# A fused sequence model on one core: the attention core rewritten with values computed first and all loops unrolled

## What is computed

```python
q = x @ Wq; k = x @ Wk; v = x @ Wv
attn = softmax(einsum('btd,bTd->btT', q, k) * scale)        # within each 64-token sequence
attn_out = einsum('btT,bTd->btd', attn, v) @ Wp + bp
cms_out = gelu(attn_out @ cW1 + cb1) @ cW2 + cb2 + target_embed
modifier = gelu(concat([attn_out, cms_out]) @ mW1 + mb1) @ mW2 + mb2
out = clip(x + cms_out + modifier, 0, 1)
```

## Time and profile before

| | us |
|---|---|
| median of 3 runs (2616.24 to 2621.03) | 2616.32 |
| profiled execution, its time | 2620.1 |
| profiled execution, its span | 2618.4 |
| TensorE busy | 2477.1 (95%) |
| TensorE weight loads busy | 2049.8 (78%) |
| VectorE busy | 1048.2 (40%) |
| ScalarE busy | 922.3 (35%) |
| GpSimd busy | 377.6 (14%) |

### The profile page before, as it was taken

The page is one execution under the profiler, slowest core; times in us unless marked ns, Lnnn a source line. Parts: engine busy times, 40 slices in busy tenths (PEclk is TensorE's granted clock), DMA queues, the critical chain, the costliest instruction groups (busy, mean ns, idle before and its releaser), DMA issues. The chain is left out here.

```text
span 2618.4 us, 29174 instructions
## 1 busy us (share of the span) xinstructions
PE 2477.1 (95%) x11376; PEld 2049.8 (78%) x11376; DVE 1048.2 (40%) x1434; ACT 922.3 (35%) x1242; POOL 377.6 (14%) x294
## 2 busy tenths in 40 slices
PE   5888999999999999999999999998999999969995
PEld 4765788888878888888788888887888888758884
DVE  4544333422244333222433342224333322357776
ACT  3544333322234333222334332223333222246663
POOL 2673000000000000000000000000000000029887
PEclk9999999999999999999999999999999999989997
DMA  5444011021120110211201111102111111063243
GB/s 185 153 169 177 33 48 48 32 80 48 48 81 33 50 46 33 80 48 48 97 33 48 48 71 58 48 32 81 43 41 56 50 48 50 34 225 137 81 137 129
DMA packets 41676, 195.64 MB, mean 75 GB/s; under 512 B 5746, under 2 KB 5746, under 8 KB 24836
## 3 DMA queue, kind: packets, MB, share of 16 engines
q1 hardware_dynamic: 35844, 152.68, 16.8%
q0 software_dynamic: 5760, 41.95, 4.0%
HBM read 163.16 MB, written 31.46 MB: 74 GB/s over the span
## 5 line engine op out<-in xcount | busy, mean ns | idle before, releaser
L1181 DVE TENSOR_TENSOR h_lo<-g,h_hi 128x512 fp32r<-128x512 f32 x256 | 177.4, 693 | 756.3 <-ACT h_hi L1089 756.3
L57 PE MATMUL bank<-h_hi,w_hiB 128*128 128x512 f32 x1152 | 449.2, 390 | 11.7 <-DVE h_lo L1158 11.7
L59 PE MATMUL bank<-h_hi,w_loB 128*128 128x512 f32 x1152 | 448.4, 389 | 0.0
L58 PE MATMUL bank<-h_lo,w_hiB 128*128 128x512 f32 x1152 | 448.2, 389 | 0.0
L1086 ACT ACTIVATE g<-bank,bias_cols 128x512 f32<-128x512 f32 x256 | 176.5, 689 | 630.0 <-PE bank L59 393.2
L59 PE MATMUL bank<-o_hi,w_loA 128*128 128x512 f32 x768 | 298.9, 389 | 0.0
L57 PE MATMUL bank<-o_hi,w_hiA 128*128 128x512 f32 x768 | 298.8, 389 | 0.0
L58 PE MATMUL bank<-o_lo,w_hiA 128*128 128x512 f32 x768 | 298.8, 389 | 0.0
L1028 ACT ACTIVATE w_hiB<-w_raw 128x2048 fp32r<-128x2048 f32 x37 | 71.0, 1920 | 565.5 <-PE bank L59 565.5
L57 PEld LDWEIGHTS bank<-h_hi,w_hiB 128*128 128x128 f32 x1152 | 216.2, 188 | 58.2 <-issue 6.7
L59 PEld LDWEIGHTS bank<-h_hi,w_loB 128*128 128x128 f32 x1152 | 216.2, 188 | 45.5
(11 more groups left out here) (210 smaller groups left out, 4213.8 us busy)
## 6 DMA issues: line engine op xcount, KB each, us to landing
w_raw<-in_units_a SPq DMA_DIRECT2D x32, 1024.0 KB, 4.8
w_raw<-in_units_b SPq DMA_DIRECT2D x32, 1024.0 KB, 4.8
w_raw<-in_units_c SPq DMA_DIRECT2D x16, 1024.0 KB, 4.8
w_raw<-in_w_packed SPq DMA_DIRECT2D x30, 512.0 KB, 4.1
w_raw<-in_rows_packed SPq DMA_DIRECT2D x20, 512.0 KB, 4.5
x_tok<-x SPq DMA_DIRECT2D x16, 512.0 KB, 6.6
x<-stage SPq DMA_DIRECT2D x32, 256.0 KB, 2.8
first_gain<-in_rows_packed SPq DMA_DIRECT2D x10, 512.0 KB, 4.5
```

The costliest lines, as they stand in the source:

```text
L57: pe.matmul(out, lh, rh, start=(i == 0), stop=False)
L58: pe.matmul(out, lh, rl, start=False, stop=False)
L59: last = pe.matmul(out, ll, rh, start=False, stop=(i == len(terms) - 1))
L1181: v.tensor_tensor(h_lo[:, j, cols(n)], g[q % 2][:], h_hi[:, j, cols(n)].bitcast(F32), ALU.subtract).then_inc(hlo_done, 1)
```

## The change

The core computes the same. What differs:

- **Values first.** The product with `fold_v` is taken of the transposed input, tile by tile (`value`, eight product tiles per block, tokens as rows), and ScalarE evicts each result over the token tile in `x_tok`. `attend` then multiplies these values with the probabilities, and its result is the output itself: `a_hi`, `a_lo` and the output product go, and `attended` makes `o_hi` and `o_lo`.
- **Order on TensorE.** Value tiles stand between queries, scores and the transposes of the probabilities; both halves are attended one behind the other.
- **Next block.** In the last chunk of blocks 0 to 2, the next block's 32 transposes stand among the output tiles (after the first and after the fourth) and use banks 0 to 3 only; transposes 4 to 7 wait for the low halves of tiles 0 to 3. Query 0 of the next block follows the output tiles, then four of the eight tiles of final transposes, the first value tile, and the other four. Final transposes use banks 4 to 7, and wait for all accumulations. The query waits for the low halves of all eight tiles.
- **Raw input.** It is evicted to `xr`, in the space of `o_hi`, because `acc` is still in use. GpSimd copies it to `acc` when the final transposes of the block before are done; ScalarE waits for these copies before it writes `o_hi`.
- **Queues.** On ScalarE and VectorE the evictions and splits of the next block stand in the last chunk, between the splits of slots A, C and B. On SyncE the stores of a block stand behind the first two weight loads of the next block; the wait for a block's stores moves to VectorE, ahead of the first hidden chunk. In block 3 the last three weight loads and splits, which nothing uses, are left out.
- **Loops.** All hardware loops of the core are unrolled, and addresses are constants.

The core of the diff, with what stays the same left out:

```diff
+    V_BANK = (0, 1, 5, 6, 0, 1, 2, 3)
+    S_BANK = (4, 7)
...
+        xr = sb("xr", [P, KD, SBT], at=places["o_hi"])
...
-        a_hi = h_hi[:].rearrange("p k n -> p (k n)")[:, 0:KD * 512].rearrange("p (k n) -> p k n", k=KD)
-        a_lo = h_lo[:].rearrange("p k n -> p (k n)")[:, 0:KD * 512].rearrange("p (k n) -> p k n", k=KD)
...
-        probsT = sb("probsT", [P, HT, P])
+        probsT = [sb(f"probsT{n}", [P, HT, P]) for n in range(NH)]
...
+            def store(s):
+                for t in range(TT):
+                    sp.wait_ge(fin_done, TT * s + t + 1)
+                    sp.dma_start(dst[s * SBT + t * P:s * SBT + (t + 1) * P, :], stage[:, t, :]).then_inc(stored[t % 2], 16)
...
+            for s in range(SB):
+                more = s < SB - 1
                 load_a(s, 1, units_a[0])
                 load_bc(s, 1, 1, units_b[0])
+                if s:
+                    store(s - 1)
                 for c in range(CH):
                     load_a(s, 2 + c, units_a[1 + c])
                     load_bc(s, 2 + c, 1, units_b[1 + c])
                 for c in range(CH):
+                    if c < CH - 1 or more:
+                        load_a(s, 2 + CH + c, units_a[1 + CH + c] if c < CH - 1 else fold_m)
+                        load_bc(s, 2 + CH + c, 1 + c, units_c[(c + 1) % CH])
+                        load_bc(s, 2 + CH + c, 2 + c, units_b[1 + CH + c] if c < CH - 1 else fold_v)
                     if more and c == 0:
                         sp.wait_ge(sum_ready, TILES * s + TILES)
                         load_x(s + 1)
...
+            def transposes(s, tiles):
+                for t in tiles:
                     if t % XT == 0:
                         pe.wait_ge(x_in[t // XT], 16 * s + 16)
+                    if t >= 4:
+                        pe.wait_ge(xlo_done, TT * s + t - 3)
+                    elif s:
+                        pe.wait_ge(gelu_done, HTILES * s - 3 + t)
                     for k in range(KD):
+                        last = pe.transpose(bank[t % 4][:, k * P:(k + 1) * P], x_tok[:, t, k * P:(k + 1) * P], ident[:])
                     last.then_inc(tr_done, 1)
+            def query(s, n):
+                pe.wait_ge(lo_done["A"], NA * s + 1)
+                pe.wait_ge(xlo_done, TT * s + TT)
+                if n:
+                    pe.wait_ge(v_done, TT * s + 2)
+                for m in range(KD):
+                    product(pe, bank[m][:], unit_terms("A", m, xc_hi, xc_lo, n)).then_inc(y_mm, 1)
+            def value(s, t):
+                pe.wait_ge(lo_done["B"], NBU * s + 1)
+                if t < 2:
+                    pe.wait_ge(y_done, TILES * s + t + 1)
+                elif t >= 4:
+                    pe.wait_ge(y_done, TILES * s + KD + t - 3)
+                elif s:
+                    pe.wait_ge(fin_done, TT * s - 4 + t)
+                product(pe, bank[V_BANK[t]][:], [((xc_hi[:, k, tile(t)], xc_lo[:, k, tile(t)]),
+                                                  (w_hi["B"][:, k, :], w_lo["B"][:, k, :])) for k in range(KD)])\
+                    .then_inc(v_mm, 1)
+            def scores(s, n):
+                pe.wait_ge(y_done, TILES * s + KD * (n + 1))
+                if s:
+                    pe.wait_ge(fin_done, TT * s - 3 + 3 * n)
+                for i in range(HT):
+                    for k in range(KD):
+                        last = pe.matmul(bank[S_BANK[n]][:, tile(i)], yT[:, k, tile(i)], xr[:, k, tile(HT * n + i)],
+                                         start=(k == 0), stop=(k == KD - 1))
+                last.then_inc(s_mm, 1)
+            def turn_probs(s, n):
+                pe.wait_ge(probs_done, 2 * NH * s + 2 * (n + 1))
+                for i in range(HT):
+                    last = pe.transpose(bank[S_BANK[n]][:, tile(i)], probs[:, i, :], ident[:])
+                last.then_inc(pt_mm, 1)
+            def attend(s, n):
+                pe.wait_ge(pt_done, NH * s + n + 1)
+                pe.wait_ge(v_done, TT * s + TT)
+                for k in range(KD):
+                    for i in range(HT):
+                        last = pe.matmul(bank[4 * n + k][:, tile(i)], x_tok[:, HT * n + i, tile(k)],
+                                         probsT[n][:, i, :], start=True, stop=True)
+                    last.then_inc(av_mm, 1)
...
+            def finish(s, tiles):
+                pe.wait_ge(acc_done, HTILES * (s + 1))
+                for t in tiles:
+                    if t >= 4:
+                        pe.wait_ge(fin_done, TT * s + t - 3)
                     for m in range(KD):
...
+            transposes(0, range(TT))
+            query(0, 0)
+            value(0, 0)
+            for s in range(SB):
+                value(s, 1)
+                scores(s, 0)
+                query(s, 1)
+                value(s, 2)
+                value(s, 3)
+                scores(s, 1)
+                turn_probs(s, 0)
+                for t in range(4, TT):
+                    value(s, t)
+                turn_probs(s, 1)
+                attend(s, 0)
+                attend(s, 1)
+                for c in range(CH):
+                    condition(s, c)
+                    out_tiles(s, c, range(TILES))
+                for c in range(CH, 2 * CH - 1):
+                    mix(s, c)
+                    out_tiles(s, c, range(TILES))
+                c = 2 * CH - 1
+                mix(s, c)
+                if s < SB - 1:
+                    out_tiles(s, c, range(1))
+                    transposes(s + 1, range(4))
+                    out_tiles(s, c, range(1, 4))
+                    transposes(s + 1, range(4, TT))
+                    out_tiles(s, c, range(4, TILES))
+                    query(s + 1, 0)
+                    finish(s, range(4))
+                    value(s + 1, 0)
+                    finish(s, range(4, TT))
+                else:
+                    out_tiles(s, c, range(TILES))
+                    finish(s, range(TT))
...
+            def valued(s, t):
+                act.wait_ge(v_mm, TT * s + t + 1)
+                act.activation(x_tok[:, t, :], bank[V_BANK[t]][:], ACT.Copy).then_inc(v_done, 1)
...
+            def attended(s, n):
+                for k in range(KD):
+                    act.wait_ge(av_mm, TILES * s + KD * n + k + 1)
+                    act.activation(o_hi[:, k, cols(n)], bank[4 * n + k][:], ACT.Identity, bias=bp[:, k:k + 1]).then_inc(ohi_done, 1)
...
+                valued(s, 0)
+                valued(s, 1)
+                softmax(s, 0)
+                queried(s, 1)
                 split("A", NA * s + 2)
+                valued(s, 2)
+                valued(s, 3)
+                turned(s, 0)
+                softmax(s, 1)
+                for t in range(4, TT):
+                    valued(s, t)
+                turned(s, 1)
+                act.wait_ge(acc_init, KD * s + KD)
+                attended(s, 0)
+                attended(s, 1)
                 split("B", nb + 3)
...
+                for c in range(CH):
+                    chunk(s, c + CH)
+                    if c < CH - 1:
+                        split("A", NA * s + c + 3 + CH)
+                        split("C", nb + 2 * c + 4 + CH)
+                        act.wait_ge(out_mm, HTILES * s + TILES * (c + CH) + TILES)
+                        split("B", nb + 2 * c + 5 + CH)
+                    elif s < SB - 1:
+                        split("A", NA * s + c + 3 + CH)
+                        transposed(s + 1, range(4))
+                        split("C", nb + 2 * c + 4 + CH)
+                        transposed(s + 1, range(4, TT))
+                        act.wait_ge(out_mm, HTILES * s + TILES * (c + CH) + TILES)
+                        split("B", nb + 2 * c + 5 + CH)
+                        queried(s + 1, 0)
...
+                softmax(s, 0)
                 split("A", NA * s + 2)
+                softmax(s, 1)
+                attended(s, 0)
+                attended(s, 1)
                 split("B", NBU * s + 2)
...
+                    accumulate(s, c, cms, range(TILES))
                     split("B", NBU * s + c + 3)
                 for r in range(TILES):
                     n, m = r // KD, r % KD
                     v.wait_ge(chi_done, TILES * s + r + 1)
                     v.tensor_tensor(xc_lo[:, m, cols(n)], cms[:, m, cols(n)], xc_hi[:, m, cols(n)].bitcast(F32),
                                     ALU.subtract).then_inc(clo_done, 1)
...
+                for c in range(CH):
+                    hidden_lo(s, c + CH)
+                    if c == 0:
+                        v.wait_ge(sum_ready, TILES * s + TILES)
+                    if c < CH - 1:
+                        split("A", NA * s + c + 3 + CH)
+                        split("C", NC * s + c + 2)
+                        accumulate(s, c + CH, acc, range(TILES))
+                        split("B", NBU * s + c + 3 + CH)
+                    elif s < SB - 1:
+                        accumulate(s, c + CH, acc, range(1))
```

(39 more changed lines are left out.)

410 lines of the change are left out of this document (138 added, 272 removed).

## The result

| | before | after |
|---|---|---|
| median, us | 2617.33 (2616.24 to 2621.03, 4 runs) | 2589.72 (2584.97 to 2591.79, 4 runs) |
| profiled execution, time and span, us | 2620.1, 2618.4 | 2588.8, 2586.7 |
| TensorE busy, us | 2477.1 | 2471.1 |
| VectorE, ScalarE, GpSimd busy, us | 1048.2, 922.3, 377.6 | 1023.1, 902.0, 400.2 |
| instruction packets of queue q8 | 52 | 91 |

The ratio is 0.9889, 95% interval 0.9872 to 0.9907: 1.1% faster. A later comparison with more runs (the same kernel again, 2587.36 against 2618.47 us) gave 0.9883, 0.9868 to 0.9898.

The account below looks back on a forecast made before the run. TensorE was taken as fully busy mid-block, with time to win only at block passages, attention and the core's start and end. Terms 12.9 + 19.6 - 3.3 + 2.9 = 32.1 us, taken from 2616.32, gave 2584 us, range 2576 to 2597.

Parts of the forecast that it names:

- A: Passage between two blocks, three times: 64 transposes move among matmuls, 11.85 us becomes about 7.3; 4.3 us won each.
- B: Inside attention, four times: value products fill TensorE's waits; 5.7 us lost less 0.8 charged, 4.9 us won each.
- C: Start of the core, once: four banks and a wait for all eight tiles delay the first query by 3.3 us.
- D: End of the core, once: the unused split of slot B goes, so stores and what follows start 2.9 us earlier.
- E: Loops of the core: unrolling them adds nothing to the sum; the outer jump costs at most 0.4 us.
- The hand walk: Work order followed: 63.4 us from first query to first hidden product, one wait of about 0.3 us.
- new waits on ScalarE: Evictions, a split and probabilities share ScalarE's queue and hold scores or attention 3 us a block: 2596 us; chance 0.10.
- rival 4: Added GpSimd copies hold VectorE 4 us a block in the clipping, so value product and transposes slip: 2600 us; chance 0.03.
- rival 5: Some wait orders the new work behind the old, leaving only the gain at the core's end: 2613 us; chance 0.03.

Follow-up runs that it names:

- old passage: Values first and unrolled loops of the changed kernel, but the passage between blocks as before the change, with eight transpose banks: 2599.39 us, ratio to before 0.9921.
- unrolled alone: The kernel before the change with every hardware loop of the core unrolled and nothing else: 2619.04 against 2618.47 us, ratio 1.0001.
- Late splits: The changed kernel with block 0's splits of slots B and C moved behind the evictions and splits of its input tiles; four banks stay: 2585.75 us.
- attended product by bank: The changed kernel, but the first attended product waits for the value evictions bank by bank instead of for all eight: 2586.76 us.

## Why the prediction was right

The forecast stood on idle time read from a timeline, and that is where the gain came from. By its own terms (the measured ones are of the profiled executions):

| term | forecast, us | measured, us | by |
|---|---|---|---|
| A, passage, each of three | 4.3 | 4.9 | 11.85 - 6.96; 6.96 is the old passage's 11.79 less 506.46 - 501.63 |
| B, attention, each of four | 4.9 | 5.5 | 64.84 - 59.37; old passage |
| C, start of the core | -3.3 | -4.35 | 12.95 - 8.6 |
| D, end of the core | 2.9 | 2.3 | 21.25 - 18.95 |
| E, loops | 0 | 0 | unrolled alone |
| outside the core | 0 | -3.1 | 238.7 - 235.8, and 0.2 at the end |
| sum | 32.1 | 31.55 | 31.7 between the two spans |

The measured terms add up to 14.7 + 22.0 - 4.35 + 2.3 - 3.1 = 31.55.

**What was luck.** The sum is nearer than its terms. A and B were too small by 4.2 us together, C and D too large by 1.65, and the stages outside the core, which the change doesn't touch, took 3.1 us more in the profiled execution of after. The core alone won 34.7 us by its marks, 2.6 more than forecast. That the span came out within 1 us of the 2586 worked out is therefore luck; that the gain lies in A and B, and is of this size, is not. Each of the passages with the attention behind it became 10.4 us shorter, where the prediction names 9.2.

**A and B** were right in place, and both a little small, because a group of small records takes less time than I charged. In B, I took 3.84 us less 0.16 for a group of 32. Measured from its start to the start of what follows, the first scores take 3.49 us (771.30 to 774.79), the second 3.56, and the two groups of attended products 7.14 (807.09 to 814.23): 14.2 us instead of 14.7, so more of the 64.84 us was lost time. That is most of what B was short by. In A, 16 transposes take 1.67 us from start to start (738.80 to 740.47), so 6.7 for the 64 instead of 7.0; and I had rounded the 4.5 us down to 4.3. The hand walk held: 63.4 us forecast from first query to first hidden product, 62.8 measured; one wait, forecast 0.3, measured 0.34. The four idle times that I listed for B leave out the 0.25 us of 785.33, which I counted among the restarts; the sum doesn't change by it.

**C** was the right step with the size 1 us off. About 0.4 us came before it: VectorE's first low half starts 6.36 us after the first transposes, where it was 5.98. Another 0.4 came from the clock: the second four tiles' transposes ran at a granted clock of 0.54 and took 3.40 us instead of 1.9, and ScalarE can start on the first of these tiles after 0.87 us instead of 0.5. The slow part of the first query, which the bounds of the term allowed to move either way, cost 1.65 us in both profiled executions and so dropped out; in the other trace of the changed kernel it cost 2.9. Late splits show a thing that the step missed: behind the splits stands the input load, which bounds the start as soon as they are out of its way.

**D**: clipping starts 1.44 us after the last accumulation (forecast 1.3), 2.8 us earlier relative to the output product. Only 2.3 of it reach the second FFN. From the start of the clipping to GpSimd's first instruction of the new stage it takes 8.3 us (2254.45 to 2262.74) instead of 7.5. Most of the difference is the last store of the core, which lands 2.9 us after its issue instead of 2.3. All nine traces with values first have this 2.9 or 3.0, with four or eight banks at the end and with the unused loads left out or kept, and the unrolled kernel has 2.3. What makes it longer stays open.

**E**: the inner jumps cost nothing that a trace shows, and the outer one shortens the wait for the clipping by 0.2 to 0.6 us but the passage by less than 0.1 us, inside A.

**The median**, 2589.7 against 2584 forecast, lies further off than the span. I took the gain of a profiled execution from a median of three runs that was 3.8 us below the profiled one. More runs of before have a median of 2618.5; with it, 2618.5 - 32.1 = 2586.4, beside 2587.4 in the larger comparison. The first four runs of after have a median 2.4 us above that one.

The rivals: new waits on ScalarE came to 0.34 us per block. The added copies (rival 4) held nobody (768.86, below). That some wait undoes the new order (rival 5) is refuted by the run with the old passage: 506.5 us from block to block, against 501.6 with the overlap and 512.05 before.

## What to carry to other kernels

Where one engine is busy through whole stretches, list its waits by place, and price a reordering as start-to-start time now minus the work of that place at its undisturbed pace; here that gave the two large terms to within an eighth before anything was built. Moving work across a stage boundary can pay twice: it also takes away the idle time behind which TensorE's clock was low in three of nine old passages (before, unrolled and old passage) and in none of the overlapped ones. Check the one instance that the new schedule makes worse (here the first block, with half of the banks): it gave back 4 us, and a special case for it was the largest repair. Unrolling by itself bought nothing.

## What the runs showed of the hardware

**The clock behind idle time is not the same each time.** The old passage leaves TensorE idle twice, with transposes between: 1.79 to 2.11 and 1.83 us in the kernel before, 1.54 to 1.56 and 1.83 us in the unrolled one and in the run with the old passage. In the kernel before, the first queries of blocks 1 to 3 ran at 1.00 (the passages take 64.8 us to the hidden product each time); the unrolled one lost 1.65 us in block 1 (66.5) and nothing in blocks 2 and 3, and in the old-passage run two of three queries had a mean of 0.86, with part of their products at 1.2 GHz. Behind idle time of 8 us in a passage of 18, all three fell. No query behind an overlapped passage did: 501.6 to 501.7 us in every one, and 501.05 with the attended product by bank. At the start of the core the 48 products of the changed kernel's first query ran at a mean granted clock of 0.86 in one execution and at 0.78 in the other, where they took 1.3 us more (13.9 instead of 12.6). The Trainium skill ("TensorE: Matmul & The Clock Gate", Part 1: The HAM clock gate) calls the length of the slow part run-variable; the traces agree, with 0 or 1.6 us for the same waits.

**GpSimd copies and VectorE's splits hold each other.** Two timelines of after, VectorE's and then GpSimd's:

```profile
817.04 2.65 DVE L1128 TENSOR_TENSOR w_loB<-w_raw,w_hiB 128x2048 fp32r<-128x2048 f32 x1 [1.06 <-ACT w_hiB L1030]
819.80 1.33 DVE L1174 TENSOR_TENSOR h_lo<-g,h_hi 128x512 fp32r<-128x512 f32 x1
821.37 0.69 DVE L1174 TENSOR_TENSOR h_lo<-g,h_hi 128x512 fp32r<-128x512 f32 x1 [0.24 <-ACT h_hi L1072]
```

```profile
768.86 3.99 POOL L1253 COPY acc<-xr 128x1024 f32<-128x1024 f32 x4 [449.90 <-PE bank L984]
814.53 6.05 POOL L1256 COPY x_tok<-target_bias 128x1024 f32<-128x1024 f32 x4 [41.68 <-PE bank L930]
```

The last of the four target copies by itself:

```profile
817.49 3.09 POOL L1256 COPY x_tok<-target_bias 128x1024 f32<-128x1024 f32 x1
```

The four target copies take 6.05 us where they took 3.99. Three of them take about 1.04 us each as before; the last takes 3.09, because it now falls on a split and a hidden low half, whose two inputs both lie in SBUF. The split takes 2.65 us instead of 2.29, and the low half 1.33 instead of 0.69. The copy ends at 820.58, 0.9 us after the split (819.69), and the low half at 821.13: each ends only behind the one before it. The added copies at 768.86 meet only instructions that read PSUM, and take 3.99. The Trainium skill ("SBUF — State Buffer", SBUF: two separate sides) has this as a port pair that an instruction locks; the trace agrees, in which instructions meet and in their order. It costs nothing here, since TensorE waits for neither.
